# Pair 8's products with four kept pairs made by rows: 48 row units for ScalarE in place of 44

## The chip, the cores and the metric

The kernel runs on one core of a Trainium2 chip. The metric is the device time of one execution in microseconds (us), as the median of several runs. Engines are named as in the profile: PE is TensorE (PEld its weight loads), DVE is VectorE, ACT is ScalarE, POOL is GpSimd, SP is SyncE, which here only issues transfers.

## The reference

For each of 512 samples, 40 table rows of 64 numbers are looked up. Each of the 780 pairs (i, j) of these fields has a 64 x 64 matrix W. The product of a pair is the sum over e of (v_i W)_e (v_j)_e. The 780 results and 16 dense inputs go through a network of three layers.

```python
e = jnp.stack([tbl_0[ids[:, 0]], ..., tbl_39[ids[:, 39]]], axis=1)   # 512 x 40 x 64
viW = jnp.einsum('bpd,pde->bpe', vi, W)          # vi, vj: fields i and j of the 780 pairs
z = jnp.einsum('bpe,bpe->bp', viW, vj)           # 512 x 780
h = jnp.concatenate([z, dense_ctx], axis=1)
h = jnp.maximum(h @ W_top1 + b_top1, 0.0)        # 796 -> 512
h = jnp.maximum(h @ W_top2 + b_top2, 0.0)        # 512 -> 256
y = h @ W_top3                                    # 256 -> 1
```

## The kernel before, in words

Two fields make a *pair* of the kernel (NP = 20 of them, 128 partitions each). `x[:, k, :]` holds pair k turned, 128 numbers by 512 samples. Eight fields are looked up by a product with a one-hot matrix ("look" jobs). The other 16 pairs are gathered by POOL (L450) with samples on the partitions, and PE turns them (L614); ACT copies the turned result from the bank `t_ps` to `x` (L465). A "turn" job of pair k stands LEAD = 5 steps ahead of the first unit of pair k, FIRST[k]. Eight gathered pairs keep their unturned rows in `kept`, in two sets: KEPT = ((1, 3, 5, 7), (8, 9, 10, 11)).

The work between pairs is cut into 195 units, one per *step* s, in a list that `plan_units` writes. Each unit is one product on PE into a slot of `y_ps` (3 slots of two banks), followed by one multiplication of 128 x 1024 on DVE. There are three sorts:

- "cross" (m, k): fields of pair m with fields of pair k. PE L665: the weights stand, `x[m]` moves, 2 matmuls. DVE multiplies by `x[k]` into `prod` (L573). The sum over e lies across partitions, and so PE makes it: after every four such units (a *round*) 8 matmuls with `selector` sum them into the bank `z_ps` (L688, `sum_round`), SUM_LAG = 3 steps after the last of the four. "inner" units (L671) are for the products within four pairs; ACT copies their operand first (L479, "mix").
- "rows" (k, bt, 0): pair k with the four kept pairs of the first set, for a quarter of the samples (bt = 0 to 3). PE L654: `x[k]` stands, the weights `w_rows_sb` move, 2 matmuls, samples on the partitions. DVE multiplies by `kept` (L559). The sum over e lies along the free dimension: ACT makes it with 16 activations of 128 x 64 that have an accumulator output (L493, `sum_rows`), ROW_LAG = 2 steps later. Four such units stand for the four cross units (1, k), (3, k), (5, k), (7, k), and need no round.
- "rows" (k, bt, 1): the same with the second set, from pair 16 on; POOL makes their sums by halving (L423, L426), between its gathers.

`ROWS_FROM` says from which pair on the two sets are made by rows, and `ROW_EVERY` after how many other units the next row unit stands. Each engine goes through the steps in order. On PE a step is: its jobs (turns, the transposes of the row sums "z_turn" L622, the first layer's parts "partial" L633), then its unit, then a round if one is due. A unit waits for the product of three steps before (`prod_ready`). DVE waits for `rows_summed` before it writes over one of the 4 slots of row products, and for `rows_by_pool` before one of POOL's 2 slots. On ACT a step is: copies of the jobs, `save_bank` if a bank of 8 rounds is full (L484, `z_ps` to `z_sb`), then the sum of the row unit of two steps before. PE may not begin the next bank until it is saved (`z_saved`).

```python
            for s in range(STEPS):                       # ACT
                for job in JOBS_AT[s]:
                    ...
                if (r := round_at(s)) is not None and r % BANK_ROUNDS == BANK_ROUNDS - 1:
                    save_bank(r)
                if s - ROW_LAG in ROWED:
                    sum_rows(s - ROW_LAG)
            save_bank(ROUNDS - 1)
            copy_turn(JOBS_AT[STEPS][0])
```

After the last step PE goes on with the first layer: its part from the fourth saved bank (L704), the last round, the turn of the last row sums (L622), the rest (L704), the second and the third layer (L737, L743).

Of the kernel before, what the change touches and what calls it, by code (L numbers as in the profile page):

```python
# [30 lines left out]

KEPT = ((1, 3, 5, 7), (8, 9, 10, 11))
KEPT_PAIRS = KEPT[0] + KEPT[1]
ROWS_FROM = (9, 16)
ROW_PROD_SLOTS = (4, 2)
ROW_W_SLOTS = 2
ROW_SUMS = 16

ROW_EVERY = (2.5, 1.8)

CHUNK = 8
W_SLOTS = 4
# [3 lines left out]
ROUND = 4  # L46
ROW_LAG = 2
BANK_ROUNDS = 8
# [27 lines left out]
def plan_units():  # L76
# [4 lines left out]
    for k in range(1, NP):  # L81
        own = [("cross", m, k) for m in range(k) if not any(k >= ROWS_FROM[q] and m in KEPT[q] for q in range(2))]
        if k % 4 == 3:
            own.insert(min(k, 6), ("inner", k // 4))
        units += own

    start = units.index(("cross", 0, ROWS_FROM[0]))
    before_pool = units.index(("cross", 0, ROWS_FROM[1])) - start
    behind = [[] for _ in units]
    for i in range(BT * (NP - ROWS_FROM[0])):  # L90
        k, bt = ROWS_FROM[0] + i // BT, i % BT
        at = ROW_EVERY[0] * i
        if at > before_pool:
            at = before_pool + ROW_EVERY[1] * (i - before_pool / ROW_EVERY[0])
        behind[max(start + int(at), units.index(("cross", 0, k)) + 2 * bt)].append(("rows", k, bt, 0))
    for k in range(ROWS_FROM[1], NP):
        for bt in range(BT):
# [6 lines left out]
STEPS = len(UNITS)  # L104
# [5 lines left out]
ROUNDS = -(-len(SUMMED) // ROUND)  # L110
EARLY_BANKS = 2 * PARTIAL_PAIRS
# [6 lines left out]
LAST_UNITS = len(SUMMED) - ROUND * (ROUNDS - 1)  # L118
DENSE_ROW = 16
Z_TURN_AT = ROWED[BT * GROUPS_IN_BANK - 1] + 8  # L120
assert STEPS == 195 and ROUNDS == EARLY_BANKS * BANK_ROUNDS + 2 and LAST_UNITS == ROUND - 1
ROW_COLUMNS = ROW_SUMS * (NP - ROWS_FROM[0] + NP - ROWS_FROM[1])
assert P < ROW_COLUMNS <= 2 * P
INNER_AT = {u[1]: s for s, u in enumerate(UNITS) if u[0] == "inner"}
# [100 lines left out]
def last_of_round(r):  # L225
    return SUMMED[min(ROUND * r + ROUND, len(SUMMED)) - 1]


def dlrm_tower(nc, ids, ids_one_hot, row_numbers, small_tables, tables, dense_t, w_units, w_rows, w1, b1, w2, b2, w3, out):
    ctx = ExitStack()  # L230
    with ctx:
# [355 lines left out]
        def _(pe):  # L587
# [88 lines left out]
            def sum_round(r):  # L676
                units = range(ROUND * r, min(ROUND * r + ROUND, len(SUMMED)))
                pe.wait_ge(prod_ready, last_of_round(r) + 1)
                if r == 0:
                    pe.wait_ge(selector_ready, 2)  # L680
                elif r % BANK_ROUNDS == 0:
                    pe.wait_ge(z_saved, r // BANK_ROUNDS)
                row = 4 * (r % BANK_ROUNDS)
                for n in range(2):
                    for u in units:
                        last = n == 1 and (r % BANK_ROUNDS == BANK_ROUNDS - 1 or r == ROUNDS - 1)
                        q = 32 * (u % ROUND)
                        ins = pe.matmul(z_ps[q:q + 32, :], selector[:, 30 - row - 2 * n:62 - row - 2 * n],  # L688
                                        prod[:, 2 * (u % G_UNITS) + n, :],
                                        start=(n == 0 and row == 0), stop=last)  # L690
                if r == ROUNDS - 1:

                    pe.wait_ge(dense_loaded, 16)
                    ins = pe.matmul(z_ps[32 * LAST_UNITS:32 * LAST_UNITS + 32, :], ident[:, 0:32], z_sb[:, BANKS - 1, :],
                                    start=False, stop=True)
                ins.then_inc(round_summed, 1)

            def first_layer(b, m):
# [9 lines left out]
            for s in range(STEPS):  # L708
                for job in JOBS_AT[s]:
                    if job[0] != "mix":  # L710
                        turn(job)
                multiply(s)
                if (r := round_at(s)) is not None:
                    sum_round(r)
            for r in range(ROUNDS - 1):
                if last_of_round(r) + SUM_LAG >= STEPS:
                    sum_round(r)
# [3 lines left out]
            for m in range(2):  # L721
                first_layer(EARLY_BANKS, m)
            sum_round(ROUNDS - 1)
            pe.wait_ge(prod_ready, STEPS)
            for m in range(2, M1):
# [8 lines left out]
            for k in range(M1):  # L734
                pe.wait_ge(h1_ready, k + 1)
                for m in range(M2):
                    ins = pe.matmul(h2_ps[m], w2_sb[:, k, P * m:P * m + P], h1_sb[:, k, :],  # L737
                                    start=(k == 0), stop=(k == M1 - 1))
# [88 lines left out]
```

## Time and profile before

| | |
|---|---|
| median of 3 runs | 346.77 us (346.64 to 347.47) |
| profiled execution, its own time | 345.37 us |
| its span | 343.6 us |
| PE busy | 326.8 us, 95% |
| DVE busy | 258.3 us, 75% |
| ACT busy | 205.9 us, 60% |
| POOL busy | 206.2 us, 60% |
| chain that ended last | PE 87%, POOL 5%, DVE 2%, issue 2% |

Busy time is the time in which at least one instruction of the engine runs, and matmuls overlap. In the profile, each matmul of the source is two records, so that a unit is "x4" and a round "x16". "Idle before" is the time that an engine stood still ahead of an instruction, with what ended it.

### The profile page before, as it was taken

The page shows a single profiled execution, that of the slowest core. Times are in us where ns is not written, and L with a number is a line of the kernel's source. Part 1 is how long each engine was busy: PE and PEld are TensorE (multiplying, and loading weights), DVE is VectorE, ACT ScalarE, POOL GpSimd, SP SyncE. Part 2 cuts the span into 40 slices and gives each one's busy share as a digit, 9 for nine tenths or more (in the row PEclk, how much of TensorE's full clock was granted, in tenths as well). Part 3 has the DMA queues.
Part 4 walks back from the last instruction along what each step waited for, and adds up shares of the span by engine and source line. Part 5 has one row for each costly group of instructions (what it writes and reads, how often), then busy time and mean ns, then how long its engine had stood idle before and what let it go on. Part 6 is the DMA issues. An engine that isn't in the chain of part 4 may idle for free.

```text
span 343.6 us, 5753 instructions
## 1 busy us (share of the span) xinstructions
PE 326.8 (95%) x1618; PEld 110.8 (32%) x1618; DVE 258.3 (75%) x271; ACT 205.9 (60%) x1467; POOL 206.2 (60%) x357
## 2 busy tenths in 40 slices
PE   0999879999999999999999999999999999999997
PEld 0333223323333332333333333333333333323342
DVE  3967599177878898877868688999978797799230
ACT  1010400120009799969886799799869758979432
POOL 2888888888871876654444444388888864257000
DMA  6941121413311373123412030304011010000000
GB/s 205 404 176 25 21 84 27 142 27 86 84 22 65 67 287 107 22 82 104 135 42 77 8 110 11 101 13 131 14 42 39 6 31 0 2 1 1 0 3 0
DMA packets 12466, 24.10 MB, mean 70 GB/s; under 512 B 3969, under 2 KB 3969, under 8 KB 12306
## 3 DMA queue, kind: packets, MB, share of 16 engines
q1 hardware_dynamic: 8338, 19.53, 16.2%
q0 software_dynamic: 4096, 4.20, 6.3%
q8 instruction: 13, 0.21, 0.2%
q14 instruction: 19, 0.16, 0.2%
HBM read 23.72 MB, written 0.00 MB: 69 GB/s over the span
## 4 chain that ended last, share of the span: by engine, by line
PE 87%; POOL 5%; DVE 2%; issue 2%; DMA 1%; ACT 1%; SPq 1%; POOLq 0%; DVEq 0%
PE y_ps L665 33%; PE z_ps L688 17%; PE y_ps L654 15%; PE t_ps L595 7%; PE t_ps L633 4%; PE y_ps L704 3%; POOL row_prod_pool L423 3%; PE t_ps L614 2%; PE y_ps L737 2%; PE y_ps L595 2%; POOL rows L450 2%; DMA table<-in_small_tables 1%; PE y_ps L671 1%; DVE prod L573 1%; DVE one_hot L538 1%
## 5 line engine op out<-in xcount | busy, mean ns | idle before, releaser
L573 DVE TENSOR_TENSOR prod<-y_ps,x 128x1024 f32<-128x1024 f32 x130 | 154.0, 1216 | 45.1 <-PE y_ps L665 44.7
L493 ACT ACTIVATE row_prod<-row_prod 128x64 f32<-128x64 f32 x704 | 168.4, 242 | 20.9 <-DVE row_prod L559 20.9
L665 PE MATMUL y_ps<-x,w_sb 64*128 64x512 f32 x520 | 131.9, 612 | 5.8 <-ACT x L465 2.3
L493 ACT ACTIVATION_READ_ACCUMULATOR row_prod<-row_prod 128x1 f32 x704 | 132.6, 188 | 0.0
L450 POOL DMA_INDIRECT rows<-in_tbl,ids_sb x64 | 61.1, 954 | 64.2 <-PE y_ps L665 30.2
L450 POOL DMA_INDIRECT kept<-in_tbl,ids_sb x64 | 62.0, 968 | 22.1 <-POOL spacer L441 17.1
L665 PEld LDWEIGHTS y_ps<-x,w_sb 64*128 64x128 f32 x520 | 45.2, 185 | 81.7 <-issue 40.1
L688 PE MATMUL z_ps<-prod,selector 128*32 128x512 f32 x540 | 65.4, 598 | 0.0
L654 PE MATMUL y_ps<-w_rows_sb,x 64*128 64x512 f32 x240 | 64.8, 620 | 0.1
L423 POOL TENSOR_TENSOR row_prod_pool<-row_prod_pool 128x512 f32<-128x512 f32 (+4 forms) x80 | 48.5, 606 | 23.5 <-DVE row_prod_pool L559 17.9
L559 DVE TENSOR_TENSOR row_prod<-y_ps,kept 128x1024 f32<-128x1024 f32 x44 | 53.5, 1216 | 8.3 <-PE y_ps L654 8.3
L465 ACT ACTIVATE x<-t_ps 128x512 f32<-128x512 f32 x18 | 10.6, 588 | 81.2 <-PE t_ps L614 42.6
L654 PEld LDWEIGHTS y_ps<-w_rows_sb,x 64*128 64x128 f32 x240 | 20.1, 185 | 35.2 <-issue 17.9
L441 POOL MEMSET spacer<- 128x128 f32 x127 | 30.6, 241 | 0.2
L538 DVE TENSOR_SCALAR one_hot<-x,numbers 128x512 f32<-128x512 int32 x64 | 27.5, 499 | 4.2 <-DMA x<-in_ids_one_hot 4.2
L595 PE MATMUL t_ps<-one_hot,table 128*64 128x512 f32 x96 | 23.0, 634 | 7.9 <-DMA table<-in_small_tables 7.9
L688 PEld LDWEIGHTS z_ps<-prod,selector 128*32 128x32 f32 x540 | 14.2, 109 | 46.2 <-issue 30.2
L559 DVE TENSOR_TENSOR row_prod_pool<-y_ps,kept 128x1024 f32<-128x1024 f32 x16 | 19.5, 1219 | 5.1 <-PE y_ps L654 2.5
L633 PE MATMUL t_ps<-z_sb,w_sb 128*128 128x512 f32 x32 | 15.9, 618 | 0.0
L595 PEld LDWEIGHTS t_ps<-one_hot,table 128*64 128x64 f32 x96 | 7.3, 146 | 22.5 <-issue 21.6
L479 ACT ACTIVATE x_mix<-x 64x512 f32<-64x512 f32 x20 | 12.6, 628 | 0.5
L704 PE MATMUL y_ps<-z_sb,w_sb 128*128 128x512 f32 (+1 forms) x24 | 11.0, 601 | 0.0
(45 smaller groups left out, 88.9 us busy)
## 6 DMA issues: line engine op xcount, KB each, us to landing
w_sb<-in_w_units SPq DMA_DIRECT2D x17, 512.0 KB, 3.5
w_rows_sb<-in_w_rows SPq DMA_DIRECT2D x15, 256.0 KB, 3.9
x<-in_ids_one_hot SPq DMA_DIRECT2D x8, 256.0 KB, 4.4
table<-in_small_tables SPq DMA_DIRECT2D x8, 256.0 KB, 6.1
w_sb<-in_w SPq DMA_DIRECT2D x1, 1792.0 KB, 8.7
kept<-in_tbl,ids_sb POOLq DMA_INDIRECT x64, 2.5
rows<-in_tbl,ids_sb POOLq DMA_INDIRECT x64
w_sb<-in_w SPq DMA_DIRECT2D x1, 512.0 KB
```

The lines of the kernel that those rows point to most:

```text
L423: pool.tensor_tensor(prods[:, :, 0:half], prods[:, :, 0:half], prods[:, :, half:2 * half], ALU.add).then_inc(rows_halved, 1)
L441: pool.memset(spacer[:], 0.0).then_inc(spaced, 1)
L450: pool.indirect_dma_start(rows_ap(n, bt)[:, h * D:(h + 1) * D], None, tables[f], bass.IndirectOffsetOnAxis(ap=ids_sb[:, bt, f:f + 1], axis=0),
L493: ins = act.activation(own, own, ACT.Copy, accum_out=z_rows[:, bt, column:column + 1])
L538: ins = dve.tensor_scalar(one_hot[:, h, k, :], ids_all[:, 2 * n + h, :], numbers[:, k:k + 1], None, ALU.is_equal)
L559: dve.tensor_tensor(row_prod[q][:, n % ROW_PROD_SLOTS[q]], y_ps[:, s % Y_SLOTS], leaf.to_broadcast([P, 2, B]), ALU.mult).then_inc(prod_rea ...
L573: dve.tensor_tensor(prod[:, at:at + 2, :], y_ps[:, s % Y_SLOTS], leaf, ALU.mult).then_inc(prod_ready, 1)
L595: ins = pe.matmul(dst[D * h:D * h + D, :], table[:, n, h, k, :], one_hot[:, h, k, :], start=(k == 0), stop=(k == TK - 1))
L633: ins = pe.matmul(dst, w1_sb[:, b, P * m:P * m + P], z_sb[:, b, :], start=(b % 2 == 0), stop=(b % 2 == 1))
L654: ins = pe.matmul(y_ps[:, slot, h, :], x[own, k, P * bt:P * bt + P], w_rows_sb[own, q, (k - ROWS_FROM[q]) % ROW_W_SLOTS, :], start=True, s ...
L665: ins = pe.matmul(y_ps[:, slot, h, :], w_sb[own, c % W_SLOTS, at:at + P], x[own, m, :], start=True, stop=True)
L688: ins = pe.matmul(z_ps[q:q + 32, :], selector[:, 30 - row - 2 * n:62 - row - 2 * n], prod[:, 2 * (u % G_UNITS) + n, :], start=(n == 0 and ...
```

## The change

Row units of the first set begin with pair 8 in place of pair 9, and stand a little closer: one per 2.25 other units in place of one per 2.5 until pair 16. The units (1, 8), (3, 8), (5, 8), (7, 8) leave the list, and (8, 0, 0) to (8, 3, 0) enter it. There are still 195 steps: 131 units with rounds in place of 135 (33 rounds in place of 34), and 48 row units of the first set in place of 44. The last bank of `z_ps` now gets one round, of three units, and so the matmul that brings in the dense inputs is the first to write its quarter.

```diff
-ROWS_FROM = (9, 16)
+ROWS_FROM = (8, 16)
...
-ROW_EVERY = (2.5, 1.8)
+ROW_EVERY = (2.25, 1.8)
...
-assert STEPS == 195 and ROUNDS == EARLY_BANKS * BANK_ROUNDS + 2 and LAST_UNITS == ROUND - 1
+assert STEPS == 195 and ROUNDS == EARLY_BANKS * BANK_ROUNDS + 1 and LAST_UNITS == ROUND - 1
...
                     ins = pe.matmul(z_ps[32 * LAST_UNITS:32 * LAST_UNITS + 32, :], ident[:, 0:32], z_sb[:, BANKS - 1, :],
-                                    start=False, stop=True)
+                                    start=True, stop=True)
```

The steps of everything behind pair 8 follow from these numbers. On PE, from the round of step 30 on, before the change (a unit is x2 here, a round x8, a turn x4):

```order
L688 MATMUL z_ps<-prod,selector 32x512 x8
L665 MATMUL y_ps<-x,w_sb 128x512 x4
L614 MATMUL t_ps<-ident,kept 128x128 x4
L665 MATMUL y_ps<-x,w_sb 128x512 x4
L688 MATMUL z_ps<-prod,selector 32x512 x8
L665 MATMUL y_ps<-x,w_sb 128x512 x8
L688 MATMUL z_ps<-prod,selector 32x512 x8
L654 MATMUL y_ps<-w_rows_sb,x 128x512 x2
L614 MATMUL t_ps<-ident,kept 128x128 x4
```

And from the same round on, after the change:

```order
L688 MATMUL z_ps<-prod,selector 32x512 x8
L614 MATMUL t_ps<-ident,kept 128x128 x4
L654 MATMUL y_ps<-w_rows_sb,x 128x512 x2
L665 MATMUL y_ps<-x,w_sb 128x512 x4
L654 MATMUL y_ps<-w_rows_sb,x 128x512 x2
L665 MATMUL y_ps<-x,w_sb 128x512 x2
L688 MATMUL z_ps<-prod,selector 32x512 x8
L665 MATMUL y_ps<-x,w_sb 128x512 x2
L654 MATMUL y_ps<-w_rows_sb,x 128x512 x2
L614 MATMUL t_ps<-ident,kept 128x128 x4
L665 MATMUL y_ps<-x,w_sb 128x512 x4
```

The next rounds stand at steps 34 and 38 before and at 35 and 41 after; the turns of pairs 9 and 10 stand at steps 31 and 38 in place of 33 and 40, and row units are among the cross units from step 31 on in place of 39.

Further on PE, from the round of step 145 on, before the change (L622 is the z_turn, L633 a part of the first layer):

```order
L688 MATMUL z_ps<-prod,selector 32x512 x8
L665 MATMUL y_ps<-x,w_sb 128x512 x2
L654 MATMUL y_ps<-w_rows_sb,x 128x512 x2
L665 MATMUL y_ps<-x,w_sb 128x512 x2
L614 MATMUL t_ps<-ident,rows 128x128 x4
L654 MATMUL y_ps<-w_rows_sb,x 128x512 x2
L665 MATMUL y_ps<-x,w_sb 128x512 x2
L654 MATMUL y_ps<-w_rows_sb,x 128x512 x4
L665 MATMUL y_ps<-x,w_sb 128x512 x2
L688 MATMUL z_ps<-prod,selector 32x512 x8
```

And from the round of step 137 on, after the change:

```order
L688 MATMUL z_ps<-prod,selector 32x512 x8
L665 MATMUL y_ps<-x,w_sb 128x512 x2
L654 MATMUL y_ps<-w_rows_sb,x 128x512 x4
L622 MATMUL t_ps<-ident,z_rows 128x128 x4
L665 MATMUL y_ps<-x,w_sb 128x512 x4
L654 MATMUL y_ps<-w_rows_sb,x 128x512 x4
L633 MATMUL t_ps<-z_sb,w_sb 128x512 x2
L665 MATMUL y_ps<-x,w_sb 128x512 x2
L688 MATMUL z_ps<-prod,selector 32x512 x8
```

The z_turn moves from step 157 to step 141, and the four parts of the first layer from steps 161, 165, 173 and 177 to steps 145, 153, 157 and 161: 32 row units are done sooner. The first four parts move from steps 79, 88, 92 and 102 to 87, 91, 102 and 106.

At the end of ACT's list, before the change (L493 is one activation of a row sum, so that x16 is one row unit; L484 saves a bank; L468 is the copy of the last row sums):

```order
L493 ACTIVATE row_prod,z_rows<-row_prod 128x64 x16
L484 ACTIVATE z_sb<-z_ps 128x512
L493 ACTIVATE row_prod,z_rows<-row_prod 128x64 x48
L484 ACTIVATE z_sb<-z_ps 128x512
L468 ACTIVATE z_sb<-t_ps 112x512
```

And after the change:

```order
L493 ACTIVATE row_prod,z_rows<-row_prod 128x64 x48
L484 ACTIVATE z_sb<-z_ps 128x512
L493 ACTIVATE row_prod,z_rows<-row_prod 128x64 x16
L484 ACTIVATE z_sb<-z_ps 128x512
L468 ACTIVATE z_sb<-t_ps 128x512
```

The fourth bank is full at step 193 in place of 185, so that its save stands right ahead of the last row unit's sum, and two row units later than before.

## Rows read from the trace of the kernel before

**Rows 1.** Page, busy time, share of the span and instructions

```profile
PE 326.8 (95%) x1618; PEld 110.8 (32%) x1618; DVE 258.3 (75%) x271; ACT 205.9 (60%) x1467; POOL 206.2 (60%) x357
```

**Rows 2.** Windows: us, then busy us of PE, PEld, DVE, ACT, POOL

```profile
89.40:101.20 11.80, 11.80 (x74) 4.08 (x70) 9.00 (x9) 1.20 (x2) 9.42 (x17) 1.00 0.26 67
...
101.20:215.70 114.50, 114.50 (x604) 39.26 (x602) 91.82 (x81) 98.48 (x743) 57.40 (x98) 1.00 0.27 84
```

**Rows 3.** Timeline of PE about step 39: start us, us, what

```profile
99.32 1.92 PE L688 MATMUL z_ps<-prod,selector 128*32 128x512 f32 x16
101.18 1.13 PE L654 MATMUL y_ps<-w_rows_sb,x 64*128 64x512 f32 x4
102.24 0.66 PE L614 MATMUL t_ps<-ident,kept 128*128 128x128 f32 x4
102.83 1.99 PE L665 MATMUL y_ps<-x,w_sb 64*128 64x512 f32 x8
```

**Rows 4.** Timeline of PE, steps 138 to 145, a run of eight units

```profile
239.88 1.13 PE L665 MATMUL y_ps<-x,w_sb 64*128 64x512 f32 x4
240.85 1.02 PE L654 MATMUL y_ps<-w_rows_sb,x 64*128 64x512 f32 x4
241.71 1.02 PE L665 MATMUL y_ps<-x,w_sb 64*128 64x512 f32 x4
...
244.67 1.13 PE L654 MATMUL y_ps<-w_rows_sb,x 64*128 64x512 f32 x4
245.80 1.13 PE L665 MATMUL y_ps<-x,w_sb 64*128 64x512 f32 x4
...
247.99 1.93 PE L688 MATMUL z_ps<-prod,selector 128*32 128x512 f32 x16
```

**Rows 5.** Groups of ACT from 101.2 to 215.7 us; two starts of row sums

```profile
L493 ACT ACTIVATE row_prod<-row_prod 128x64 f32<-128x64 f32 x362 | 86.6, 242 | 9.6 <-DVE row_prod L559 9.6
...
L479 ACT ACTIVATE x_mix<-x 64x512 f32<-64x512 f32 x8 | 5.0, 628 | 0.2
...
103.71 0.26 ACT L493 ACTIVATE row_prod<-row_prod 128x64 f32<-128x64 f32 x1 [0.18 <-DVE row_prod L559]
...
107.59 0.26 ACT L493 ACTIVATE row_prod<-row_prod 128x64 f32<-128x64 f32 x1
```

**Rows 6.** Timeline of DVE: a run of four units, and a wait for POOL

```profile
126.62 3.47 DVE L573 TENSOR_TENSOR prod<-y_ps,x 128x1024 f32<-128x1024 f32 x3
130.02 1.21 DVE L559 TENSOR_TENSOR row_prod<-y_ps,kept 128x1024 f32<-128x1024 f32 x1
...
253.51 1.22 DVE L559 TENSOR_TENSOR row_prod_pool<-y_ps,kept 128x1024 f32<-128x1024 f32 x1 [1.19 <-POOL z_rows L426]
```

**Rows 7.** Instructions on `kept`: ns min/median/max, first and last start us; landing

```profile
L450 POOL DMA_INDIRECT kept<-in_tbl,ids_sb x64: 952/952/1188, 6.5 to 101.3; - x64
...
DMA to landing us min/median/max: 2.3/2.5/3.9
```

**Rows 8.** Timelines of PE and of ACT at the end of the steps

```profile
306.77 1.92 PE L688 MATMUL z_ps<-prod,selector 128*32 128x512 f32 x16
...
316.74 1.92 PE L688 MATMUL z_ps<-prod,selector 128*32 128x512 f32 x16
318.60 1.13 PE L665 MATMUL y_ps<-x,w_sb 64*128 64x512 f32 x4
319.66 1.98 PE L704 MATMUL y_ps<-z_sb,w_sb 128*128 128x512 f32 x4
...
325.24 0.60 PE L622 MATMUL t_ps<-ident,z_rows 128*112 128x128 f32 x4
...
308.76 0.60 ACT L484 ACTIVATE z_sb<-z_ps 128x512 f32<-128x512 f32 x1 [1.40 <-PE z_ps L688]
...
316.90 0.24 ACT L493 ACTIVATE row_prod<-row_prod 128x64 f32<-128x64 f32 x1
...
320.48 0.24 ACT L493 ACTIVATE row_prod<-row_prod 128x64 f32<-128x64 f32 x1
```

## The prediction

> **What bounds the kernel now.** The page's busy line comes first: PE is busy 95% of the span, DVE 75%, ACT and POOL 60% [rows 1]. Busy matmuls overlap, so that 95% by itself proves nothing; the timeline of PE does. There I read starts, not durations. A round begins at 99.32 and the next unit at 101.18: 1.86 us. That unit, alone between a round and a turn, holds PE 1.06 us, and the turn 0.59 [rows 3]. In a run of units the one behind a round takes 0.97 and the next 0.86 [rows 4]. So PE's list is a sum: 0.86 for a unit, 1.85 for a round, 0.59 for a turn, and 0.20 for each place where a run of units is broken (0.10 on the unit ahead of it and 0.10 on the one behind). In the windows from 89.4 to 215.7 PE has no idle time at all, while DVE works 100.8 of 126.3 us [rows 2]. PE bounds this stretch.
>
> There is one thing beside it. DVE needs 1.13 us for a unit in a run: four begin at 126.62, and the last of them at 130.02 [rows 6]. PE needs 0.86, and may be three units ahead. In a short run it gains a lead, and in a round DVE catches up. In a long run PE ends at DVE's pace: in the run of eight of steps 138 to 145, the units at 244.67 and 245.80 are 1.13 apart. The whole run takes 247.99 - 239.88 = 8.11 us, against 8 x 0.86 + 0.20 = 7.08: 1.03 us are lost [rows 4]. So what a round is worth depends on how long the run is that it leaves behind.
>
> **The change, part by part.**
>
> *One round less.* Four cross units give way to four row units. On PE a row unit costs what a cross unit costs: at 240.85 a row unit takes 0.86 before the next [rows 4]. DVE's multiplication has the same shape and duration (1.21 and 1.13 apart) whichever it is [rows 6]. What goes is the 34th round: -1.85 us, and its break, -0.20. **-2.05 us**, on an engine without idle time.
>
> *Breaks.* Turns and parts of the first layer break runs too, and where one falls right behind a round it breaks nothing more. Counted over steps 30 to 194 in the two orders, there are 46 places with a round or a job between two units before and 43 after. One of the three is the round's own, counted above; the turn of pair 9, for one, stood inside a run and now stands behind a round. **-0.40 us** for the other two.
>
> *Longer runs.* One round less among the same 195 units makes runs longer. By the length of runs between rounds or parts of the first layer, and with the run of eight at 1.03 lost, one of four or fewer loses nothing, since PE is at most three units ahead. Between these I take 0.2 for five, 0.5 for six and 0.75 for seven, and less where a turn (0.59) falls in the run. From step 31 to 119 there are now eight runs of six (three of them without a turn) where there were six (one without), and six of five as before: about +0.9. Behind step 161 the parts of the first layer are gone, and a run of eight with a turn and one of seven stand where runs of one to five stood: +1.3. Against these stand steps 120 to 160. Before, they hold runs of seven, nine, eight, eight and seven, with a wait of DVE for POOL of 1.19 us in the fourth [rows 6]; POOL has 2 slots and is late there with its sums. At 1.03 for the plain run of eight I put the five at 4.9. After, the z_turn and three parts of the first layer fall there, which let both DVE and POOL catch up, and leave runs of seven, eight, seven and seven, three of them with a turn in the run: 2.3. That is -2.6. The net of the three is **-0.4**. Its bounds are +0.9 (the middle gains half as much) and -1.2 (a turn in a run of six to eight saves all of its 0.59).
>
> *ScalarE.* Four more row sums. A sum is 3.88 us from start to start with a wait, 16 activations 0.24 apart [rows 5]; in a chain 3.84. Four of them are 15.4 us, at no cost if ACT has the time. It worked 98.5 of 114.5 us between steps 39 and 120 [rows 2], with 24 sums. Now there are 28 between steps 31 and 120. The rest there is 8 copies of turns, 4 copies of parts and 2 saves at 0.60 [rows 8], and 8 activations of "mix" at 0.63 [rows 5]: 13.4 us. That makes 28 x 3.84 + 13.4 = 120.9 us. The time is 11.8 + 114.5 - 2.05 = 124.2 [rows 2]. So ACT goes from 86% to 97% in this stretch. It still fits, and a queue that is late by some us costs nothing as such. DVE waits for a sum only when four row units are outstanding, over 11 us late. PE waits for the copy of a turned pair, which stands behind a sum, only 5 steps (over 5 us) after the turn. The worst places are the two "mix" jobs, four activations in a row (2.5 us) between two sums; each makes the sums behind it some 2.5 us late, under the 5 us that are free. **0**; bound +5 (below, as a rival).
>
> The Trainium skill (ScalarE: Activation LUTs, section What ACT_TABLE_LOAD costs) prices an activation with immediate scale and bias at 186 ns + 0.833 ns per element, with 93 ns of overlap back to back. For 64 elements that would be 239 ns each, in agreement with the 242 of the trace, but 146 ns apart. By it a row sum would be 2.3 us and ACT at 64% in this stretch. The trace has them 0.24 us apart, with the accumulator's read in between, and the measurement decides.
>
> *Gathers.* The turn of pair 10 comes at step 38 in place of 40, with one round fewer ahead of it: 102.24 [rows 3] - 1.85 - 2 x 0.96 = 98.5. Its eight gathers are the 49th to 56th of 64 that are evenly spread from 6.5 to 101.3, 1.505 apart [rows 7]: the last starts at 89.3 and has landed by 93.2 at the slowest. Pair 11 lands by 105.2 at the slowest; its turn is 9 units, 2 rounds and a turn later, at 98.5 + 0.59 + 7.7 + 3.7 + 0.4 = 110.9. Nothing waits: **0**.
>
> *Loads.* SP now waits for later row units ahead of some loads; the weights of a row unit are still asked for 14 or more steps ahead, and land in 4 us. The load of the first layer's weights comes some 12 us later, 25 us ahead of its use. **0.**
>
> *The end.* The save of the fourth bank now stands behind the round of step 193, and PE's first L704 waits for it. Times are those of before: the round starts at 316.74. ACT's earlier save began 1.99 us behind the start of its round (306.77 to 308.76) and takes 0.60 [rows 8]. So this one ends at 319.33, and PE reaches L704 at 319.66 [rows 8]: 0.3 us to spare. The last row sum, from 316.90 to 320.7 before, must wait for the save and ends at about 323.2; the L622 that needs it comes at 325.24 [rows 8]: 2 us to spare. **0**, with a bound of +0.5 if the save is late.
>
> **Sum.** -2.05 - 0.40 - 0.40 = -2.85 us. The profiled execution would go from a span of 343.6 to 340.8 and from 345.37 to 342.5. The runs before have a median of 346.77, 1.4 above it; moved by the same -2.85 they give **343.9 us**.
>
> **The rivals.**
>
> *A. As summed:* 343.9, own range 343.2 to 344.9 by the bounds of the runs' term and the end.
>
> *B. The time goes into waits for VectorE.* Then PE only looks full, and the round that goes was a pause in which DVE caught up. For it: DVE's 1.13 against PE's 0.86, and 1.03 lost in a run of eight [rows 4, 6]. Against it: over the stretch that loses the round, DVE works 100.8 of 126.3 us [rows 2], so that only single runs can be bound by it. Were each of the eight runs of six and the two late ones to have one more unit at DVE's pace than I gave them, 10 x (1.13 - 0.86) = 2.7 of the gain would go and 0.15 stay: 346.6. The Trainium skill (Perfetto Trace Analysis, section Identifying the Most-Contended Engine) warns of this: matmul busy share is a poor measure of how near the limit TensorE is, and the busy share of the weight loads, here 32% [rows 1], is better. By that rule PE would have room and B would hold. The starts in [rows 3] have no gap, and speak against it.
>
> *C. ScalarE becomes the bound: slower.* At 97% between steps 31 and 120 it has 3.3 us in hand. If a row sum took x in place of 3.84, it would be late by 28x + 13.4 - 124.2 at the end of the stretch, of which about 4 us are free (the five steps of a turned pair). To end more than 1 us above before it must lose 3.9 us, which asks for x = 4.25, 11% more. At 4.3 the time would be 343.9 + 5.6 = 349.5. Against it: 704 activations have a mean of 242 ns, and nothing in the change touches them. The queue's clumps could act alike, and that is the likelier way.
>
> *D. A load or gather is late* at one of the places above: 1 to 2 us, 345 to 346.
>
> **Chances.** A 0.82, B 0.08, C 0.04, D 0.06. A measurement of this kernel tells about 0.3% (1.04 us) from no change. Faster by more than that: A and half of D and a little of B, 0.87. Within it: 0.09. Slower: C, 0.04. The range reaches from 343.0, where the runs' term is at its better bound, to 345.3, which takes in the worse bound of that term with the end's and half of D.
>
> **What would show it.** PE's records of L688 should go from 540 to 524, and its busy time fall by some 2 us. DVE's waits for POOL L426 (1.19 us and smaller ones) should vanish between steps 138 and 160. ACT should be busy at over 95% from about 90 to 214 us, with no row sum starting more than 3 us behind its product. L704 should follow the last unit without idle time. The forecast is wrong if PE shows idle time ahead of units that waits for ACT `x` L465 (C), or if starts in the runs of six are spread over more than 6.0 us (B).

## The result, and the profile after

| | before | after |
|---|---|---|
| median of 8 runs, us | 346.62 (345.55 to 347.88) | 343.36 (342.22 to 345.13) |
| ratio, 95% interval | | 0.9892 [0.9867, 0.9918] |
| profiled execution, its own time, us | 345.37 | 343.4 |
| its span, us | 343.6 | 341.6 |

The change makes the kernel faster: by 3.3 us from median to median, by 3.7 us (2.8 to 4.6) by the ratio. A second comparison, made later, gave 343.29 against 346.88, 0.9896 [0.9862, 0.9930].

The page of after: busy time of each engine (answers to [rows 1]), the chain that ended last by engine, and groups of instructions (busy us, mean ns of one, idle time before them and what ended it).

```profile
PE 325.0 (95%) x1602; PEld 110.6 (32%) x1602; DVE 258.6 (76%) x271; ACT 221.2 (65%) x1595; POOL 206.2 (60%) x357
...
PE 93%; DVE 2%; issue 2%; DMA 1%; ACT 1%; SPq 1%; DVEq 0%
...
L493 ACT ACTIVATE row_prod<-row_prod 128x64 f32<-128x64 f32 x768 | 183.7, 242 | 15.5 <-DVE row_prod L559 15.3
...
L688 PE MATMUL z_ps<-prod,selector 128*32 128x512 f32 x524 | 63.5, 598 | 0.0
...
L559 DVE TENSOR_TENSOR row_prod_pool<-y_ps,kept 128x1024 f32<-128x1024 f32 x16 | 19.5, 1217 | 1.3 <-PE y_ps L654 1.3
```

L688 has 524 records, one round of 16 fewer. POOL, 5% of the chain before, is gone from it, and no DVE product waits for POOL any more. ACT has 15 us more to do, and the mean of one activation is still 242 ns.

Where the time is, I read from the starts of units on PE:

| | before | after | difference |
|---|---|---|---|
| step 30 starts at, us | 86.60 | 87.76 | +1.16 |
| steps 30 to 119, us | 129.13 | 127.59 | -1.54 |
| steps 120 to 193, us | 102.86 | 101.27 | -1.59 |
| step 194 to L622, us | 6.64 | 6.64 | 0.00 |

Nothing in front of step 30 changed on PE. In the profiles of this study that ran without a pause there (more on it below), step 30 starts anywhere between 86.6 and 89.9 us: this is the scatter between executions. From step 30 on, after is 3.13 us shorter. The 1.16 of step 30 is why the two profiled executions differ by only 2.0 us.

The stretch that the prediction spoke of most, steps 138 to 161. PE of before, a run of eight units and the next one (the first run of eight is in [rows 4]):

```profile
249.85 1.13 PE L665 MATMUL y_ps<-x,w_sb 64*128 64x512 f32 x4
...
252.62 0.66 PE L614 MATMUL t_ps<-ident,rows 128*128 128x128 f32 x4
253.21 1.13 PE L654 MATMUL y_ps<-w_rows_sb,x 64*128 64x512 f32 x4
254.79 1.13 PE L665 MATMUL y_ps<-x,w_sb 64*128 64x512 f32 x4 [0.45 <-DVE row_prod_pool L559]
...
259.33 1.92 PE L688 MATMUL z_ps<-prod,selector 128*32 128x512 f32 x16
```

The same engine after:

```profile
239.85 1.13 PE L665 MATMUL y_ps<-x,w_sb 64*128 64x512 f32 x4
240.81 1.88 PE L654 MATMUL y_ps<-w_rows_sb,x 64*128 64x512 f32 x8
242.63 0.66 PE L622 MATMUL t_ps<-ident,z_rows 128*128 128x128 f32 x4
243.21 1.99 PE L665 MATMUL y_ps<-x,w_sb 64*128 64x512 f32 x8
245.03 1.88 PE L654 MATMUL y_ps<-w_rows_sb,x 64*128 64x512 f32 x8
246.85 1.98 PE L633 MATMUL t_ps<-z_sb,w_sb 128*128 128x512 f32 x4
248.76 1.13 PE L665 MATMUL y_ps<-x,w_sb 64*128 64x512 f32 x4
249.82 1.92 PE L688 MATMUL z_ps<-prod,selector 128*32 128x512 f32 x16
```

Both runs have eight units. Before, 259.33 - 249.85 = 9.48 us hold 8 x 0.86 and the break (7.08) and a turn with its break (0.79): 1.61 are lost, part of it in a wait that ends with DVE's `row_prod_pool`, the product that waited 1.19 for POOL [rows 6]. After, 249.82 - 239.85 = 9.97 hold 7.08, the z_turn with its break (0.79) and a part of the first layer with its break (1.91 + 0.20): 9.98. Nothing is lost, nor is anything in the next run of eight, which holds a turn and a part too (261.64 - 251.68 = 9.96):

```profile
251.68 1.13 PE L665 MATMUL y_ps<-x,w_sb 64*128 64x512 f32 x4
...
261.64 1.92 PE L688 MATMUL z_ps<-prod,selector 128*32 128x512 f32 x16
```

The two jobs, 2.50 us of work, stand where PE would have waited.

Jobs that moved there are missing further on. After, steps 171 to 177 are a run of seven with no job in it:

```profile
287.76 1.99 PE L665 MATMUL y_ps<-x,w_sb 64*128 64x512 f32 x8
...
292.64 1.13 PE L665 MATMUL y_ps<-x,w_sb 64*128 64x512 f32 x4
293.77 1.13 PE L654 MATMUL y_ps<-w_rows_sb,x 64*128 64x512 f32 x4
294.83 1.92 PE L688 MATMUL z_ps<-prod,selector 128*32 128x512 f32 x16
```

It takes 7.07 us against 7 x 0.86 + 0.20 = 6.22, and its last units are again 1.13 apart: 0.85 lost, where before two parts of the first layer stood among these steps and nothing was lost.

The end came as forecast (start, us, what; [rows 8] before). First PE, then the save on ACT:

```profile
314.77 1.92 PE L688 MATMUL z_ps<-prod,selector 128*32 128x512 f32 x16
316.62 1.13 PE L665 MATMUL y_ps<-x,w_sb 64*128 64x512 f32 x4
317.68 1.98 PE L704 MATMUL y_ps<-z_sb,w_sb 128*128 128x512 f32 x4
...
323.26 0.60 PE L622 MATMUL t_ps<-ident,z_rows 128*128 128x128 f32 x4
...
316.76 0.60 ACT L484 ACTIVATE z_sb<-z_ps 128x512 f32<-128x512 f32 x1 [2.41 <-PE z_ps L688]
```

The save ends at 317.36, 0.3 us before L704 needs it, and the last row sum ends at about 321.2, 2 us ahead of its L622.

### The profile page after: what moved, and what is told of

Its sections match the earlier page's. It is cut to its first block, busy times and chain, and to the rows that moved or that the text cites. A ratio compares the mean times of both kernels' runs of the same rounds, so it can differ in the third digit from the quotient of the medians.

```text
span 341.6 us, 5852 instructions
## 1 busy us (share of the span) xinstructions
PE 325.0 (95%) x1602; PEld 110.6 (32%) x1602; DVE 258.6 (76%) x271; ACT 221.2 (65%) x1595; POOL 206.2 (60%) x357
## 4 chain that ended last, share of the span: by engine, by line
PE 93%; DVE 2%; issue 2%; DMA 1%; ACT 1%; SPq 1%; DVEq 0%
PE y_ps L665 34%; PE y_ps L654 18%; PE z_ps L688 17%; PE t_ps L595 7%; PE t_ps L633 4%; PE y_ps L704 3%; PE t_ps L614 3%; PE y_ps L737 2%; PE y_ps L595 2%; DMA table<-in_small_tables 1%; PE y_ps L671 1%; DVE prod L573 1%; DVE one_hot L538 1%; ACT x L465 1%; PE t_ps L743 1%
## 5 line engine op out<-in xcount | busy, mean ns | idle before, releaser
L493 ACT ACTIVATE row_prod<-row_prod 128x64 f32<-128x64 f32 x768 | 183.7, 242 | 15.5 <-DVE row_prod L559 15.3
L573 DVE TENSOR_TENSOR prod<-y_ps,x 128x1024 f32<-128x1024 f32 x126 | 149.8, 1217 | 44.9 <-PE y_ps L665 44.6
L493 ACT ACTIVATION_READ_ACCUMULATOR row_prod<-row_prod 128x1 f32 x768 | 144.3, 188 | 0.0
L665 PE MATMUL y_ps<-x,w_sb 64*128 64x512 f32 x504 | 129.4, 615 | 5.4 <-ACT x L465 2.3
L665 PEld LDWEIGHTS y_ps<-x,w_sb 64*128 64x128 f32 x504 | 43.3, 185 | 79.9 <-issue 37.5
L654 PE MATMUL y_ps<-w_rows_sb,x 64*128 64x512 f32 x256 | 67.2, 612 | 0.2
L559 DVE TENSOR_TENSOR row_prod<-y_ps,kept 128x1024 f32<-128x1024 f32 x48 | 58.4, 1217 | 9.9 <-PE y_ps L654 9.9
L688 PE MATMUL z_ps<-prod,selector 128*32 128x512 f32 x524 | 63.5, 598 | 0.0
L654 PEld LDWEIGHTS y_ps<-w_rows_sb,x 64*128 64x128 f32 x256 | 22.0, 185 | 35.7 <-issue 18.8
L688 PEld LDWEIGHTS z_ps<-prod,selector 128*32 128x32 f32 x524 | 13.8, 109 | 44.8 <-issue 31.9
L633 PE MATMUL t_ps<-z_sb,w_sb 128*128 128x512 f32 x32 | 15.9, 618 | 0.0
L704 PE MATMUL y_ps<-z_sb,w_sb 128*128 128x512 f32 x24 | 11.0, 601 | 0.0
```

The costliest lines, as they stand in the source:

```text
L493: ins = act.activation(own, own, ACT.Copy, accum_out=z_rows[:, bt, column:column + 1])
L559: dve.tensor_tensor(row_prod[q][:, n % ROW_PROD_SLOTS[q]], y_ps[:, s % Y_SLOTS], leaf.to_broadcast([P, 2, B]), ALU.mult).then_inc(prod_rea ...
L573: dve.tensor_tensor(prod[:, at:at + 2, :], y_ps[:, s % Y_SLOTS], leaf, ALU.mult).then_inc(prod_ready, 1)
L633: ins = pe.matmul(dst, w1_sb[:, b, P * m:P * m + P], z_sb[:, b, :], start=(b % 2 == 0), stop=(b % 2 == 1))
L654: ins = pe.matmul(y_ps[:, slot, h, :], x[own, k, P * bt:P * bt + P], w_rows_sb[own, q, (k - ROWS_FROM[q]) % ROW_W_SLOTS, :], start=True, s ...
L665: ins = pe.matmul(y_ps[:, slot, h, :], w_sb[own, c % W_SLOTS, at:at + P], x[own, m, :], start=True, stop=True)
```

## The experiments

**The theories.** *Theory R:* PE's time is a list: units, rounds, jobs and breaks at fixed prices, plus what PE loses in long runs to VectorE's pace. So the change is worth its round (2.05), two breaks (0.40) and what the new order does to the runs. *Rival N:* only the number of rounds counts, and the order gives nothing. *Rival S:* the closer spacing of the row units is the gain by itself. The prediction's B (a round is only a pause for VectorE) and C (ScalarE is nearly the bound) are tried as well.

To compare lists I take the starts of units as above; what is "lost" is the time of a stretch less 0.86 for each unit (1.02 for an inner one), 1.85 for each round, 0.59 for each turn, 1.91 for each part and 0.20 for each break. The versions were timed in four series, each beside the kernel before: e1 to e4, e5 to e8, f1 to f4, g1 to g3. In the first and the last of them PE stood still for some us about step 30, where products of DVE began late for a reason that the trace doesn't show, and the kernel before ran 7 to 13 us longer too. So their times are compared within the series, and their profiles only from step 120 on, or from step 61 where that is said.

### One part alone: the spacing, and the places of the jobs

*The spacing without the exchange* (in two series):

```diff
-ROW_EVERY = (2.5, 1.8)
+ROW_EVERY = (2.25, 1.8)
```

> The kernel before with one number of the change alone: a row unit per 2.25 other units in place of 2.5, still from pair 9 on, so 34 rounds and 44 row sums. Theory R (TensorE's list is a sum of units, rounds and jobs, plus what long runs of units lose to VectorE's pace of 1.13 us): no round goes, so the 1.85 stays; the z_turn goes from step 157 to 149 and the parts of the first layer come up to nine steps sooner, which breaks long runs of steps 140 to 175: about -1.1 us against before. Rival N (the number of rounds decides, -2.05 a round and nothing else): 0 +- 0.3. Rival S (the closer spacing itself brings the gain): the whole -3 to -3.7.

> The kernel before with one row unit per 2.25 other units, again. Theory R: 228.9 us between steps 30 and 194, with one round pushed behind step 194 (1.85), so 1.2 us less than before in all. Rival N: no difference.

Measured: 359.89 against 359.94, 0.9999 [0.9967, 1.0031]; and, in a series without that pause, 345.53 against 346.88, 0.9968 [0.9949, 0.9988]. Its list has 34 rounds, one of them behind step 194. From step 30 to L622 it takes 229.14 + 8.50 = 237.64 us, before 231.99 + 6.64 = 238.63: 0.99 less, by the order alone (forecast 1.1 and 1.2). The first comparison can't tell this from nothing; the second can. Rival N, which gives it nothing, falls, and so does S, which gives it all of the gain.

*The change with the z_turn and four parts back where they stood before* (and once more the change itself, in the same series as f2):

```diff
+JOBS_MOVED = {('z_turn', 0): 157, ('partial', 1, 0): 161, ('partial', 1, 1): 165, ('partial', 1, 2): 173, ('partial', 1, 3): 177}
...
+    for job, at in JOBS_MOVED.items():
+        for jobs in jobs_at:
+            if job in jobs:
+                jobs.remove(job)
+        jobs_at[at].append(job)
```

> The changed kernel with the z_turn and the second four parts of the first layer held at the steps that they had before (157; 161, 165, 173, 177), all else as changed. Theory R: the runs of eight of steps 140 to 160 come back, with VectorE's wait for GpSimd, and the late runs of eight and seven go: about +1.1 us against the changed kernel, so -2 against before. Rival N (only the round counts): no difference from the changed kernel, within 0.3 us.

> The changed kernel itself, beside its variants on one chip. Between the starts of the units of steps 30 and 194 its profile showed 228.9 us against 232.0 before, a gain of 3.1; whatever the time gains beyond that lies in the look-ups before step 30, which the change does not touch, and is scatter. So -3.1 +- 0.5 us against before. If there is more in the change than the steps show: -3.7 or more again.

> The changed kernel with z_turn and the last four parts at the steps of before, again, since in the first profile TensorE's clock fell for some 10 us about step 30. Theory R: 229.9 us between steps 30 and 194, 1.1 more than the changed kernel. Rival N (only the round counts): 228.9.

Measured: 358.33 against 359.94, 0.9965 [0.9938, 0.9993]; then 345.30, 0.9958 [0.9934, 0.9981], where the change itself had 343.29. In the list steps 30 to 193 take 230.31 us against 228.86 and 228.85 in the two profiles of the change: +1.45 for the same work in another order (forecast +1.1). The run that held the z_turn and a part holds neither now, and the next one has DVE wait for POOL again. PE, steps 138 to 161 (L673 and L662 are the units L665 and L654, L696 is the round L688):

```profile
240.29 1.13 PE L673 MATMUL y_ps<-x,w_sb 64*128 64x512 f32 x4
...
248.49 1.93 PE L696 MATMUL z_ps<-prod,selector 128*32 128x512 f32 x16
...
256.55 2.17 PE L662 MATMUL y_ps<-w_rows_sb,x 64*128 64x512 f32 x8 [0.86 <-DVE row_prod_pool L567]
```

The first run takes 8.20 us, 1.12 over its list. So nearly half of the change's gain in the list hangs on where five jobs that it never names come to stand.

### Jobs spread over the long runs

If a job in a long run costs less than its own time, all nine movable ones should stand so. The same edit with other steps, on the change (shown here) and on the kernel before (its steps are in e4's expectation):

```diff
+JOBS_MOVED = {('partial', 0, 0): 101, ('partial', 0, 1): 120, ('partial', 0, 2): 127, ('partial', 0, 3): 135, ('z_turn', 0): 143, ('partial', 1, 0): 158, ('partial', 1, 1): 175, ('partial', 1, 2): 182, ('partial', 1, 3): 190}
```

> The changed kernel with its nine late jobs put into the long runs of units: parts of the first layer at steps 101, 120, 127, 135 and 158, 175, 182, 190, the z_turn at 143. No work is added or taken away. Theory R: each such job gives VectorE 1.9 us to catch up where TensorE would wait for it; the stalls fall from about 8 us to 5, -3.1 us against the changed kernel and -6 against before. Rival N: no difference from the changed kernel, or slower, since the last jobs stand next to the end.

> The kernel before, 34 rounds, with its late jobs in its own long runs: 108, 126, 135, 142 and 165, 174, 182, 190, the z_turn at 159. Theory R: -5.5 us against before, and only some 0.6 us slower than the changed kernel with spread jobs: a round that stands where VectorE must catch up anyway is worth much less than 2.05. Rival N: no difference from before within 0.5 us, and 2 to 3 us slower than the changed kernel with spread jobs.

> The changed kernel with its jobs in the long runs, again for a profile without the fall of the clock. Theory R: 225.6 +- 0.4 us between steps 30 and 194, 3.1 less than the changed kernel, and 6 us below before in time. Rival N: 228.9.

> The kernel before, 34 rounds, with its jobs in its long runs, again for a profile without the fall of the clock. Theory R: 226.2 +- 0.4 us between steps 30 and 194, 5.8 less than before and only 0.6 more than the changed kernel with spread jobs (225.64). If a round is worth 2.05 wherever it stands: 227.7 or more.

Measured on the change: 354.69 against 359.94, 0.9842 [0.9805, 0.9879]; and 339.51 against 346.88, **0.9807 [0.9769, 0.9845]**, the best version of the study, with the same work as the change. Its steps 30 to 193 take 225.64 us, as Theory R had it, 3.2 less than the change's. Before, spread in the same way: 355.56, 0.9859 [0.9817, 0.9901], and 350.09 against 354.08, 0.9864 [0.9795, 0.9934]. Between the two spread versions in one series (355.56 and 354.69) lie 0.87 us, with intervals that overlap.

The last profile doesn't meet its expectation as it stands (steps 30 to 193 in 232.78 us in place of 226.2), because PE waits 2 to 3 us at a time ahead of steps 30 and 34 there. Its steps 120 to 193 don't help either: they hold ten rounds, as those of the spread change do. But the disturbance is over by step 61. From there to step 78, where the first job is missing that was moved, each unit starts as in the profile of the kernel before, to 0.01 us. So the stretch can be put together from two profiles: steps 30 to 60 of the kernel before, where the lists are the same, and steps 61 to 193 of the spread one. Step 61 in before, then steps 61 and 194 in g1 (L673 is the unit L665):

```profile
131.32 1.13 PE L665 MATMUL y_ps<-x,w_sb 64*128 64x512 f32 x4
...
141.11 1.13 PE L673 MATMUL y_ps<-x,w_sb 64*128 64x512 f32 x4
...
322.93 1.13 PE L673 MATMUL y_ps<-x,w_sb 64*128 64x512 f32 x4
```

(131.32 - 86.60) + (322.93 - 141.11) = 226.54 us, 5.45 less than before; with the profile of e4 it is 226.65. That meets the 226.2 +- 0.4 and speaks against a round that is worth 2.05 wherever it stands (227.7 or more). The spread change takes 225.64, 0.90 less, which agrees with the 0.87 of the medians. At fixed prices its round and breaks are worth 2.45; 1.55 of them are lost again in the longer runs that they leave (5.06 us lost in all, against 3.51).

### An empty round, behind a round or within a run

Four times 8 matmuls that add the products of `x` with columns 0 to 29 of `selector` to `z_ps`. These columns are zero, so the sums stay what they are. In e5 they stand right behind a real round, in e6 (steps 50, 126, 181, 189) in the middle of runs:

```diff
+DUMMY_AT = (46, 87, 104, 153)
...
+            def empty_round():
+                for n in range(2):
+                    for q in range(0, P, 32):
+                        pe.matmul(z_ps[q:q + 30, :], selector[:, 0:30], x[:, n, :], start=False, stop=False)
...
+                if s in DUMMY_AT:
+                    empty_round()
```

> The changed kernel with four more rounds on TensorE, each right behind a real one (steps 46, 87, 104, 153). They multiply zero weights with a tile that stands in the memory, wait for nothing, and nobody waits for them. Theory R: 1.85 us each, since the run is broken there already: +7.4 us in all, less at most 0.2 where VectorE still has something to catch up, read between the starts of the units of steps 30 and 194. Rival B of the prediction (TensorE only looks full): far less, as the four are then hidden.

> The changed kernel with the same four additional rounds in the middle of long runs: steps 50, 126, 181 and 189 (runs of six, seven, eight and eight units). Theory R: +5.0 us in all, 1.25 each: 2.05 with the new break, less what VectorE no longer holds up behind it. Rival N: 2.05 each, +8.2 us.

Measured: 350.98 and 347.44, one run of each, with 347.25 for one run of the kernel before (the change wasn't run in this series). Against the change's 228.86, steps 30 to 193 take 235.73 and 233.81 us, +6.87 and +4.95: 1.72 for each round behind a round (forecast 1.8 to 1.85), and 1.24 for each within a run (forecast 1.25), though it breaks the run. Here is one within a run (L711 is the empty round; L655, L666 units):

```profile
222.84 1.02 PE L655 MATMUL y_ps<-w_rows_sb,x 64*128 64x512 f32 x4
223.70 1.02 PE L666 MATMUL y_ps<-x,w_sb 64*128 64x512 f32 x4
224.66 1.92 PE L711 MATMUL z_ps<-x,selector 128*30 128x512 f32 x16
226.51 1.13 PE L655 MATMUL y_ps<-w_rows_sb,x 64*128 64x512 f32 x4
```

On PE it takes its 1.85 us, and of its 2.05 with the break 0.8 come back, on the mean of four, in the units behind it, which find `y_ps` free. Rival B falls: a pause for VectorE that costs nothing would have come back whole.

### ScalarE loaded further

One, then two more activations per row sum into a spare buffer (for two, `EXTRA = 2` and eight places in place of four):

```diff
+EXTRA = 1
...
+                        for _ in range(EXTRA if h == 0 and n == 0 else 0):
+                            act.activation(spare[:, SPARE_AT[0] % 4, :], own, ACT.Copy, accum_out=spare_sum[:, SPARE_AT[0] % 4:SPARE_AT[0] % 4 + 1])
```

> The changed kernel with 17 activations for each row sum in place of 16; the additional one writes to a tile that nobody reads. A sum takes 4.08 us in place of 3.84, and ScalarE needs 28 x 4.08 + 13.4 = 127.6 us of the 124 between steps 31 and 120. The prediction's formula, with 4 us free: no time lost. Followed sum by sum through ScalarE's queue: the first-layer part of step 87 waits 1.7 us for the copy of the turn before it, and one turned pair is 0.2 late: +1.9 us. If ScalarE had ample room: 0.

> The same with 18 activations for each row sum: 4.34 us, 134.9 of 124 us. The prediction's formula: 10.7 - 4 = +6.7 us at the end of the stretch. Followed sum by sum: +5.6 us, with TensorE waiting some 3 us for the turned pair of step 75 and 2.7 us at step 87. If ScalarE had ample room: 0.

Measured, in the list of one profile each: +0.55 and +5.88 us (345.42 and 348.61 us, one run of each). The count sum by sum had +1.9 and +5.6. Where they end in waits; first the waits of PE with 17 activations, then those of PE and one of DVE with 18 (us in total, times, longest):

```profile
PE t_ps L640 <- ACT x L469: 0.5, 1, 0.5
```

```profile
PE t_ps L640 <- ACT x L469: 2.1, 1, 2.1
PE y_ps L672 <- ACT x L469: 2.0, 1, 2.0
...
DVE row_prod L566 <- ACT row_prod L500: 1.7, 1, 1.7
```

The latest start of a sum behind its product is 2.60 us in the change (2.47 before), 3.48 and 6.05 here. At 3.84 us a sum nothing waits; at 4.08 it costs half a microsecond; at 4.32 it costs six. The formula of rival C (28x + 13.4 - 124.2, less about 4 that are free) gives 0 and, at x = 4.32, 6.2 (6.7 on record, at 4.34): it nearly has the second and misses the first, since the queue of single jobs is late at one place before it is late on the whole.

### A third slot for POOL

To see how much of the middle's loss was POOL's, in the kernel before and in the change:

```diff
-ROW_PROD_SLOTS = (4, 2)
+ROW_PROD_SLOTS = (4, 3)
```

> The kernel before with three slots in place of two for the row products that GpSimd sums; nothing else moves. If GpSimd's lateness is most of the middle term: VectorE's waits for it vanish and steps 30 to 194 take 230.0 +- 0.3 us, 2 less than before. If only VectorE's pace in long runs counts: 232.0 as before.

> The changed kernel with three such slots. There the jobs that moved already give GpSimd its time, so by both theories nothing changes: 228.86 us between steps 30 and 194, within 0.1. So the change's own worth over a kernel with three slots would be 1.1 us and not 3.1.

Measured: before with three slots 352.47 against 354.08, 0.9940 [0.9905, 0.9975]; the change with three 351.12, 0.9884 [0.982, 0.9949]. In steps 120 to 193, before goes from 102.86 to 101.12 us, and the change from 101.27 to 101.43. Lost in steps 120 to 160: 5.00 and 3.03 before, 2.11 and 2.04 after. So 2.0 of the 2.9 us that the change gains there were POOL's lateness, and the change has nothing of it left.

From step 61 to 119 both profiles start their units as those with two slots do, to 0.01 us. With the undisturbed steps 30 to 119 in front, steps 30 to 193 take 129.13 + 101.12 = 230.25 us before and 127.59 + 101.43 = 229.02 after (expected 230.0 and 228.86). So over a kernel with a third slot the change is worth 1.2 us in the list and 1.35 by the medians, whose intervals overlap: one number would have brought more than half of its gain without it.

## Why the prediction was right or wrong

| step of the sum, us | forecast | measured in the list |
|---|---|---|
| round and its break | -2.05 | -2.05 (33 rounds in place of 34, 26 for 27 in these steps) |
| two more breaks | -0.40 | -0.40 (43 for 46) |
| runs, steps 30 to 119 | +0.9 | +0.91 |
| runs, steps 120 to 160 | -2.6 | -2.89 |
| runs behind step 161 | +1.3 | +1.29 |
| runs, steps 178 to 193 | 0 | +0.01 |
| ScalarE, gathers, loads, end | 0 | 0 |
| sum | -2.85 | -3.13 |

**The kind of answer was right, the size a little small.** The forecast was 343.9, the median came out at 343.36. By the ratio, 346.62 x 0.9892 = 342.9 lies just below the range, which began at 343.0: 1.0 us under the forecast.

**The step that failed** is the net of the three terms for the runs. It was put at -0.4 and measured -0.68, inside its own bound of -1.2. The other two of the three were met to 0.01; the one that was too small is the middle's. I had put the loss there at 4.9 before and 2.3 after, "three of them with a turn in the run". It was 5.00 and 2.11: in the two runs of eight with a turn and a part, at 239.85 and 251.68, nothing at all was lost, and I had left some. The prediction had the bound for this right (a job in a run saves its own time) and chose too little of it. Plain runs of five and six lose 0.22 and 0.49 in the change, as taken (0.2 and 0.5), but those of seven 0.85 (0.75). The term behind step 161 was met to 0.01 with some luck: a run of seven cost 0.1 more there, and the run of eight with a turn 0.48, less than the 0.55 left for it.

**The rest** of the distance is not in the list, and it is the larger part. 343.9 was moved from a median of 346.77, and that of the later runs was 346.62: 0.15. Between 3.13 in the list and 3.3 (medians) or 3.7 (ratio) stay 0.1 to 0.6 us, which I can't place; the second comparison, 3.6 by either reckoning (forecast 3.1 +- 0.5), leaves 0.5. They are smaller than the ratio's interval (2.8 to 4.6) and than the scatter of step 30's start; that the change shortens anything ahead of step 30 was not shown. So the 1.0 us by the ratio are 0.28 of the runs' term, 0.15 of the median and 0.6 that stay open, and it took all three to leave the range. The prediction itself said that a measurement tells 1.04 us from no change; a range that ended on its lower side with the list's own doubt, and took nothing for this scatter, was too tight.

**The round was a real cost on PE.** Its 1.85 us was read from two starts [rows 3], and the empty rounds cost 1.72 each behind a round. That speaks against B, and against reading the weight loads' 32% as room: the Trainium skill (Perfetto Trace Analysis, section Identifying the Most-Contended Engine) holds that share for the better sign of TensorE's limit, and no such room was found here; four rounds more made steps 30 to 193 longer by 6.87 us. But a round in a run costs 1.24 of its 2.05, so B has two fifths of the truth there: what a round is worth depends on where it stands. B's own sign did not come: a plain run of six takes 5.85 us in the change, under its 6.0.

**ScalarE** took four more sums at no cost. The share forecast, 97% or at least over 95%, was too high. Window of ACT in after, its busy time in 120 us:

```profile
94.00:214.00 120.00, 113.04 (x865) 1.00 0.29 88
```

That is 94%, and 92% over all of 90 to 214 us. Of the 7 us left in this window, 2.6 are waits for products and 4.1 are waits for a part, two full banks and a turn of PE; the sum in a chain of 3.84 had neither. The latest sum starts 2.60 us behind its product, under the 3 us of the forecast. Rival C is a real mechanism with its edge between 4.08 and 4.32 us a sum (forecast: 4.25 for a slower kernel). A sum stayed at 3.84, so its 0.04 was fair.

**Waits for POOL** vanished as said, and no gather or load was late (rival D): the profile lists no wait of PE at all between steps 30 and 194. The load of the first layer's weights was issued 20 us later (139.00 for 118.73) and not 12 as the prediction had it, which cost nothing: their first use is at 164.37.

**Still open:** the 0.1 to 0.6 us beyond the list, the reason of the pauses about step 30, and the 0.24 us that both kernels with a third slot lose in steps 178 to 193. The 0.90 us between the spread kernels come from a list put together from two profiles; no single undisturbed profile of the spread kernel before shows them.

## What to carry to other kernels

On an engine that is the bound, write its time as a list of starts, and price each item by its place: in a long run, where a faster engine already waits for a slower one, an extra job or round costs less than its own time, and right behind another pause it costs nearly all of it. So put the movable work of the bound engine into its long runs: that alone, without a single instruction less, gave 3.2 us in the list and 3.8 on the chip on top of this change. A slot more for the consumer that is late (POOL here) is the other way to take the same waits, and worth trying first: one slot brought 1.7 us in the list here. And when a table of positions is computed from a parameter, read what else moves with it, since here nearly half of the gain was jobs that the diff doesn't name.

## What the hardware showed beside

- The starts on PE repeat between executions to 0.02 us over 229 us of work (steps 30 to 193: 228.86 and 228.85 in two profiles taken apart), while the look-ups ahead of them scatter by 3 us. A change of 0.3% can be read from such a stretch when the whole time can't tell it.
- PE after an idle time, in the profile of the spacing alone of the first series (e1): windows with busy us of PE, PEld, DVE, ACT, POOL, then the granted clock.

```profile
94.00:96.00 2.00, 0.00 (x0) 0.00 (x0) 0.00 (x0) 0.00 (x0) 1.46 (x4) 1.00 0.13 22
...
98.00:100.00 2.00, 2.00 (x8) 0.21 (x8) 0.85 (x1) 0.00 (x0) 1.55 (x4) 0.50 0.11 16
100.00:102.00 2.00, 2.00 (x12) 0.40 (x8) 2.00 (x3) 0.00 (x0) 1.63 (x3) 0.50 0.17 32
...
104.00:106.00 2.00, 2.00 (x12) 0.83 (x12) 1.47 (x2) 0.10 (x1) 0.00 (x0) 1.00 0.31 45
```

```profile
97.50 2.08 PE L665 MATMUL y_ps<-x,w_sb 64*128 64x512 f32 x4 [3.84 <-issue]
99.51 3.64 PE L688 MATMUL z_ps<-prod,selector 128*32 128x512 f32 x16
103.08 2.20 PE L665 MATMUL y_ps<-x,w_sb 64*128 64x512 f32 x8
```

  PE had stood still for 3.84 us before 97.50. Then the granted clock was 0.50, the lower of its two levels (1.2 GHz), and one round took 3.57 us (99.51 to 103.08) in place of 1.85. It was back at 1.00 from 104 us on. So an idle time of PE there costs more than its own length.
